# A first stage re-timed on three engines, the last root on GpSimd, and a one-sided closing test

## The chip, the cores and the metric

The kernel runs on one core of a Trainium2 chip. The metric is device time in microseconds (us) of one launch. The engines are PE (TensorE, matmuls), ACT (ScalarE), DVE (VectorE), POOL (GpSimd) and SP (SyncE, which only issues DMAs here). Each has a queue of its own and runs it in order; they meet at semaphores.

## The reference

There are 3125 nodes of 256 features and, with self loops, 53125 edges sorted by target. Cut to what matters (gates i, c, o; f is not used by the result):

```
z   = layernorm(x)                               # 3125 x 256
h   = z @ W_gnn + b_gnn                          # "lines"
x1  = x + segment_sum(h[src], dst) / max(deg, 1)
z2  = layernorm(x1)
xi, xg, xo = z2 @ U_i + b_i, z2 @ U_c + b_c, z2 @ U_o + b_o
# one sequence of 3125 nodes: c' = h*c + sigmoid(xi + h V_i) * tanh(xg + h V_c)
#                             h' = sigmoid(xo + h V_o) * tanh(c')
out = x1 + hs
```

## The kernel before, in words

The 3125 nodes are 25 blocks (steps) of 125 chunks. The recurrence is run on all 125 chunks at once, 25 steps a round, each chunk starting from a guess that the steps before it have made good; at the end a test says whether the last round has moved any start state by more than `STATE_TOL`, and only if it has does a slow exact path run. It does not run here.

The work falls into stages.

1. **Before the first turn**: edges are found, the GNN weight is scaled, PE does dummy matmuls (`keep_busy`).
2. **First stage**, a loop of turns j from 0 to 27 (`BLOCKS + 3`), written out on each engine. In turn j PE transposes block j of z (L1258), makes up to eight counts of edges from one-hot tiles (`count`, L1238), does the products of line j-2 (one matmul for the bias, L1275, six at L1278), and, for a line whose low part ACT makes, subtracts the high part of line j-3 in PSUM (L1284). ACT makes z of the next block (`first_norm`, L899; POOL, L757, makes blocks 11, 13, 15, 17, 19 and from 20 on), copies the transposed z out as its high part (L963), copies two groups of counts out (L934), then writes the low part of line j-3 (L919) and the high part of line j-2 (L914). DVE subtracts to get the low part of the transposed z (`zT_low`, L1716), compares indices to make one-hot tiles (`one_hots`, L1691, used three turns later), and does the moments of x, the roots and the edge keys in chosen turns. "Low parts by DVE" (`low_by_dve`) are lines 21 to 24: DVE takes PSUM minus the high part and PE has no subtraction to do. Edge keys are placed by DVE in turns 4 and 8 and turned by PE at the end of turns 5 and 11.
3. **Sums and gates**, places w from 0 to 649: PE multiplies counts by lines (L1244, L1246), counts the next windows, turns z2 (L1304), makes the gate inputs (L1328) and early steps of the recurrence (L1356). DVE makes the one-hots, up to six tiles ahead of PE (`RING`), then x1, its moments, z2 and the low parts of the weights (L1884, at the places in `UV_LOW`). The inverse root of the variance is made by POOL (`root`, four linked operations from L787 to L791) for turns 0 to 23, and by DVE itself (`last_root`, eight linked operations from L1785) for turn 24. Then come steps 21 to 24 and the last gates, by hand-written places (`LAST_AT`, `LATE_PARTS`).
4. **The recurrence**, 41 steps in two halves, about 1.5 us a half (L1436, L1085, L1908, L1099, L1913).
5. **The end**: the closing test (difference of cells, of states, their squares, one compare with a sum, from L1962 to L2014), the last outputs (L1972), and the last store.

The line that joins most of the engines in the first stage is this wait of PE before the products:

```
t = j - 2
if 0 <= t < BLOCKS:
    pe.wait_ge(zT_ready, t + 1)
    ...
    elif t >= 2:
        pe.wait_ge(line_low_act, lows_act(t - 2))
```

## Time and profile before

| | us |
|---|---|
| median of 3 runs | 456.59 |
| lowest, highest | 456.39, 458.94 |
| the profiled execution, its own time | 457.81 |
| its span, first to last instruction | 455.9 |
| PE, DVE, ACT, POOL busy | 416.8, 341.6, 321.5, 145.9 |

The profiled execution took 1.9 us more than its span shows, and 1.2 us more than the median. Busy shares are means over stages with different limits, so the rows further down are taken stage by stage.

### The profile page before, as it was taken

What the parts mean: (1) busy time and instruction counts of PE and PEld (TensorE: products, weight loads), DVE (VectorE), ACT (ScalarE), POOL (GpSimd) and SP (SyncE); (2) the same over time, 40 slices, a digit from 0 to 9 for tenths busy, and PEclk for the clock granted to TensorE, in tenths of its full rate; (3) what the DMA queues carried; (4) which work ended last, traced back from release to release, by engine and by line L of the source; (5) the groups of instructions that cost most, each with busy time, mean ns of one, the idle gap of its engine ahead of it and who ended that gap; (6) DMA issues with size and microseconds to landing.
All of it is one profiled execution on the core that took longest, in us unless ns stands there. A gap on an engine that the chain in (4) does not pass through costs nothing.

```text
span 455.9 us, 15425 instructions
## 1 busy us (share of the span) xinstructions
PE 416.8 (91%) x6114; PEld 368.5 (81%) x6114; DVE 341.6 (75%) x1095; ACT 321.5 (71%) x906; POOL 145.9 (32%) x249
## 2 busy tenths in 40 slices
PE   4987899999999999999999999998888889999992
PEld 3666787878898999899998989887777778888882
DVE  4989887996997868777786833627577778888885
ACT  1668696577776767667676853564788888888881
POOL 6740420153432435233422412312123222322320
PEclk9989799999999999999999999999999999999997
DMA  8375001331100001000100010000000000210112
GB/s 186 70 156 140 0 1 51 104 104 31 58 2 1 1 4 55 1 2 1 58 2 1 2 39 20 0 3 22 38 4 4 4 3 4 61 51 12 61 60 62
DMA packets 9603, 16.90 MB, mean 37 GB/s; under 512 B 2006, under 2 KB 7451, under 8 KB 9526
## 3 DMA queue, kind: packets, MB, share of 16 engines
q1 hardware_dynamic: 8230, 14.60, 11.0%
q0 software_dynamic: 880, 0.86, 0.9%
q8 instruction: 50, 0.82, 0.8%
q10 hardware_dynamic: 416, 0.39, 0.5%
q14 instruction: 27, 0.22, 0.2%
HBM read 6.23 MB, written 9.61 MB: 35 GB/s over the span
## 4 chain that ended last, share of the span: by engine, by line
PE 64%; DVE 18%; ACT 7%; issue 7%; DMA 2%; POOL 0%; SPq 0%; DVEq 0%; ACTq 0%; POOLq 0%
PE bank L1244 13%; PE bank L1246 13%; PE bank L1328 10%; PE bank L1436 9%; PE bank L1238 6%; PE bank L1356 4%; ACT tc L1099 3%; PE bank L1278 3%; DVE h L1913 3%; DVE hots L1691 3%; DVE h L1950 3%; DVE c_st L1908 2%; DMA x_sb<-in_x_dram 2%; PE bank L1472 1%; PE bank L1304 1%
## 5 line engine op out<-in xcount | busy, mean ns | idle before, releaser
L1238 PE MATMUL bank<-hots 128*128 128x125 f16 x625 | 119.7, 222 | 0.3 <-DVE hots L1691 0.2
L1691 DVE TENSOR_TENSOR hots<-iota,kp 128x1000 f16<-128x1000 f16 x160 | 106.5, 693 | 12.0 <-PE bank L1238 11.9
L1436 PE MATMUL bank<-h,V 128*128 128x62 f16 (+1 forms) x2952 | 101.1, 192 | 13.0 <-DVE h L1913 8.4
L1436 PEld LDWEIGHTS bank<-h,V 128*128 128x128 f16 x2952 | 93.0, 97 | 24.2 <-issue 22.8
L1244 PE MATMUL bank<-h_flat,counts 125*128 125x257 f16 x375 | 96.7, 273 | 0.2 <-ACT counts L934 0.2
L1246 PE MATMUL bank<-h_flat,counts 125*128 125x256 f16 x375 | 95.8, 271 | 0.0
L934 ACT ACTIVATE counts<-bank 125x500 f16<-125x500 f32 x96 | 55.2, 602 | 20.8 <-PE bank L1238 19.7
L1244 PE MATMUL bank<-h_flat,gx 125*128 125x257 f16 x250 | 68.2, 274 | 0.0
L1246 PE MATMUL bank<-h_flat,gx 125*128 125x256 f16 x250 | 67.5, 270 | 0.0
L824 POOL TENSOR_TENSOR hc<-h_flat,c_st 128x126 f32<-128x126 f32 x80 | 34.0, 425 | 95.7 <-DVE c_st L1908 84.9
L1238 PEld LDWEIGHTS bank<-hots 128*128 128x128 f16 x625 | 57.1, 98 | 7.8 <-DVE hots L1691 0.6
L1328 PE MATMUL bank<-z2T,U 128*128 128x250 f16 (+1 forms) x504 | 55.2, 258 | 1.4 <-ACT gx L986 1.1
L934 ACT ACTIVATE gx<-bank 125x500 f16<-125x500 f32 x64 | 37.3, 592 | 18.8 <-PE bank L1238 17.0
L1328 PEld LDWEIGHTS bank<-z2T,U 128*128 128x128 f16 x504 | 43.4, 97 | 6.5 <-issue 2.2
L986 ACT ACTIVATE gx<-bank,gb 128x250 f32<-128x250 f32 (+1 forms) x84 | 32.7, 443 | 22.4 <-PE bank L1328 22.3
L801 POOL TENSOR_TENSOR hc<-h,c_st 128x250 f32<-128x250 f16 x20 | 18.7, 936 | 71.6 <-DVE h L1840 69.9
L1244 PEld LDWEIGHTS bank<-h_flat,counts 125*128 125x128 f16 x375 | 36.6, 98 | 4.8 <-ACT counts L934 0.5
L1913 DVE SCALAR_TENSOR_TENSOR h<-gate,tc 128x126 f16<-128x126 f32 (+1 forms) x80 | 23.6, 294 | 20.6 <-ACT tc L1099 20.6
L787 POOL TENSOR_TENSOR rstd<-var_eps,minus_half 125x1 f32<-125x1 f32 x24 | 18.3, 764 | 63.9 <-DVE var_eps L1556 63.9
L1246 PEld LDWEIGHTS bank<-h_flat,counts 125*128 125x128 f16 x375 | 36.6, 98 | 1.7
L1099 ACT ACTIVATE tc<-c_st 128x126 f32<-128x126 f32 x82 | 25.3, 309 | 15.5 <-DVE c_st L1908 15.4
L1013 ACT ACTIVATE gate<-bank 128x500 f32<-128x500 f32 (+1 forms) x48 | 22.8, 484 | 12.6 <-PE bank L1356 11.9
(185 smaller groups left out, 781.2 us busy)
## 6 DMA issues: line engine op xcount, KB each, us to landing
h_dram<-h_flat SPq DMA_DIRECT2D x1, 3137.2 KB
x_dram<-x_sb SPq DMA_DIRECT2D x5, 625.0 KB
x_sb<-in_x_dram SPq DMA_DIRECT2D x5, 560.0 KB
out_dram<-x_sb SPq DMA_DIRECT2D x4, 560.0 KB
out_dram<-x_sb SPq DMA_DIRECT2D x1, 336.0 KB
x_sb<-in_x_dram SPq DMA_DIRECT2D x5, 65.0 KB
out_dram<-x_sb SPq DMA_DIRECT2D x4, 65.0 KB
gx<-in_L_gnn_weight_dram ACTq DMA_DIRECT2D x1, 256.0 KB, 3.8
```

Source lines behind the costliest of these rows:

```text
L824: nc.gpsimd.tensor_tensor(hc[:, q, :, 0:c1 - c0], h[:, :, c0:c1], c_st[:, c, :, c0:c1], ALU.mult).then_inc(hc_ready[q], 1)
L934: nc.scalar.activation(counts[g % 2][:, :, :, n0:n0 + n], ps_count[group % 3][0:NB, 0:n * KEYS].rearrange("p (n r t) -> p r t n", n=n, r=RUN),
L986: nc.scalar.activation(gx[:, at:at + n, m, :], gates_bank(tile // 2)[:, half * TB * NB:half * TB * NB + n * NB].rearrange("p (s k) -> p s ...
L1013: nc.scalar.activation(gate_w[:, m0:m1, :], early_bank(t, m0)[:, 0:(m1 - m0) * CHUNKS].rearrange("p (m k) -> p m k", k=CHUNKS), ACT.Tanh, ...
L1099: nc.scalar.activation(tc[:, q, :, 0:c1 - c0], c_st[:, c, :, c0:c1], ACT.Tanh, scale=0.5).then_inc(tc_ready[q], 1)
L1238: nc.tensor.matmul(ps_count[group % 3][:, pos * KEYS:(pos + 1) * KEYS], hots[:, ring, 0, g // 2, :, g % 2], hots[:, ring, 1, g // 2, 0:KEY ...
L1244: nc.tensor.matmul(sum_bank(turn)[:, 0:D + 1], of, line[:, s, D:2 * D + 1], start=(s == 0), stop=False, skip_group_check=True)
L1246: return nc.tensor.matmul(sum_bank(turn)[:, 0:D], of, line[:, s, 0:D], start=False, stop=(s == BLOCKS - 1), skip_group_check=True)
L1328: mm = nc.tensor.matmul(at_bank[:, half * TB * NB:half * TB * NB + n_blocks * NB], U16[:, w_part, d, m * P:(m + 1) * P], z2T[:, buf, z_par ...
L1436: mm = nc.tensor.matmul(to[:, m % (2 * HH) * n:(m % (2 * HH) + 1) * n], V16[:, v_part, d, m * P:(m + 1) * P], h16[:, h_part, d, c0:c1], st ...
L1691: nc.vector.tensor_tensor(hots[:, k % RING, :, :, 0:KEYS, :].rearrange("p a h n g -> p (a h) n g"), iota[:, 0:KEYS, :].unsqueeze(1).to_bro ...
L1913: return nc.vector.scalar_tensor_tensor(out=to, in0=gate[:, q, 2 * HH:MT, 0:n], scalar=1.0, in1=tc[:, q, :, 0:n], op0=ALU.add, op1=ALU.mult)
```

## The change

- **Moments sooner**: the statistics of blocks 15 to 24 go from turns 9 to 12 to turns 8 to 11, their root on ACT and DVE from turn 13 to turn 12.
- **Second keys later**: DVE places them in turn 13 (was 8), PE turns them in turn 16 (was 11). The one-hot tiles of turns 6 to 14 are dealt out anew.
- **Products one line behind**: turn 14 does lines 12 and 13, and each turn j after it line j-1. The loop ends a turn earlier. In turn 15 PE does both subtractions ahead of the products.
- **Low parts by turns**: from line 14 on the even lines are DVE's (14, 16, 18, 20, besides 21 to 24).
- **Dummy matmuls**: eight instead of one at the end of turn 4, and two more in each of turns 9 to 16, into the free half of the bank of transposed z, before PE waits for z.
- **One one-hot tile** of the next stage is made in turn 25, and the first three low parts of the weights U move from places 64, 71, 77 to 69, 74, 79.
- **Last root** on POOL like the others; the last turning of z2 on PE goes from place 635 to 632, ahead of step 24's products.
- **Closing test** of one side at a time: six compares (new plus or minus the bound against old) with a sum each, four of the cells, half by half, two of the states; PE adds the six sums. Subtractions, squares and the joint compare go. (Cells and states were squared against the bound before; now either side is tested by itself.)

The diff, cut to its core:

```
-            return t >= BLOCKS - 4
+            return t >= CATCH_UP and t % 2 == 0 or t >= BLOCKS - 4
-        PLACE_KEYS, TURN_KEYS = (4, 8), (5, 11)
+        PLACE_KEYS, TURN_KEYS = (4, 13), (5, 16)
-        HOTS_OF = [0] * HOTS_FROM + [2, 2, 1, 2, 1, 1, 1] + [2] * 11 + [0]
+        HOTS_OF = [0] * HOTS_FROM + [2, 2, 2, 2, 1, 1, 2, 0] + [2] * 10 + [0]
+        CATCH_UP = PLACE_KEYS[1] + 1
+        LINES_END = BLOCKS + 2
+        def lines_at(j):
+            if j < CATCH_UP:
+                return range(max(0, j - 2), max(0, j - 1))
+            return range(j - 2 if j == CATCH_UP else j - 1, min(j, BLOCKS))
...
# ACT, end of a turn
-                if 0 <= j - 3 and not low_by_dve(j - 3):
-                    line_low(j - 3)
-                if 0 <= j - 2 < BLOCKS:
-                    line_high(j - 2)
+                for t in lines_at(j - 1):
+                    if not low_by_dve(t):
+                        line_low(t)
+                for t in lines_at(j):
+                    line_high(t)
...
# PE, start of a turn
+                    if j >= 2:
+                        pe.wait_ge(zT_ready, j - 1)
+                    if HOTS_FROM + HOTS_LATER <= j < WARM_END:
+                        keep_busy(2 * WARM_EACH, bank[5 + j % 2][:, 2 * P:4 * P])
...
# PE, after the counts
+                lines = list(lines_at(j))
+                ahead = 0 if j == CATCH_UP + 1 else 1
+                for t in lines[:ahead]:
+                    line_products(t)
+                for t in lines_at(j - 1):
+                    if not low_by_dve(t):
+                        take_high(t)
+                for t in lines[ahead:]:
+                    line_products(t)
...
# DVE
-                if 9 <= j < 12:
-                    chunk_stats(15 + 3 * (j - 9), 18 + 3 * (j - 9))
-                if j == 12:
+                if 8 <= j < 11:
+                    chunk_stats(15 + 3 * (j - 8), 18 + 3 * (j - 8))
+                if j == 11:
...
-            UV_LOW = {64: 0, 71: 1, 77: 2, 128: 3, 152: 4, 165: 5}
+            UV_LOW = {69: 0, 74: 1, 79: 2, 128: 3, 152: 4, 165: 5}
-                if turn == BLOCKS - 1:
-                    last_root(j)
...
# the closing test on DVE
+                nc.vector.scalar_tensor_tensor(out=near_hits[:, a, :, 0:k1 - k0], in0=new[:, :, k0:k1], scalar=bound,
+                                               in1=old[:, :, k0 + 1:k1 + 1], op0=ALU.add,
+                                               op1=ALU.is_le if bound < 0 else ALU.is_ge, accum_out=near[:, a:a + 1]
+                                               ).then_inc(near_ready, 1)
```

## Rows read from the trace of the kernel before

**Rows 1.** Windows by stage: us, then each engine's busy time, PE clock, DMA share, GB/s.
```profile
26.20:56.50 30.30, 25.84 (x185) 21.26 (x184) 25.58 (x78) 22.00 (x62) 7.99 (x9) 0.83 0.38 90
56.50:72.80 16.30, 15.89 (x154) 13.50 (x152) 12.48 (x25) 16.16 (x44) 3.06 (x6) 1.00 0.01 2
72.80:107.00 34.20, 32.85 (x337) 28.74 (x338) 31.51 (x75) 21.29 (x40) 9.46 (x13) 1.00 0.32 95
107.00:300.00 193.00, 191.04 (x2028) 172.07 (x2027) 136.01 (x327) 130.21 (x289) 68.21 (x102) 1.00 0.04 15
```
**Rows 2.** Windows of 2 us in the first stage, same columns.
```profile
28.00:30.00 2.00, 2.00 (x10) 1.40 (x9) 1.59 (x3) 1.04 (x4) 0.00 (x0) 0.50 1.00 210
...
48.00:50.00 2.00, 1.80 (x9) 1.32 (x10) 1.98 (x5) 1.27 (x3) 2.00 (x3) 0.50 0.00 0
```
**Rows 3.** Waits of PE from 10 to 72 us: in total, times, longest.
```profile
PE bank L1275 <- ACT h_flat L919: 1.8, 6, 0.5
```
**Rows 4.** Timeline of PE, one steady turn (start us, us, operation).
```profile
58.60 0.37 PE L1258 MATMUL bank<-ident,gx 125*128 125x125 f32 x2
...
59.37 0.32 PE L1275 MATMUL bank<-b,ones 33*125 33x256 f16 x1
...
60.34 0.27 PE L1284 MATMUL bank<-h_flat,minus_one 125*125 125x256 f16 x1
60.45 0.38 PE L1258 MATMUL bank<-ident,gx 125*128 125x125 f32 x2
```
**Rows 5.** Timeline of ACT in the same part.
```profile
60.65 0.38 ACT L919 ACTIVATE h_flat<-bank 125x256 f16<-125x256 f32 x1
...
61.19 0.39 ACT L963 ACTIVATE gx<-bank 128x250 f16<-128x250 f32 x1
```
**Rows 6.** Timeline of DVE in the first stage.
```profile
33.43 0.28 DVE L1673 TENSOR_SCALAR gx<-gx 125x256 f32<-125x256 int32 x1
...
35.48 0.67 DVE L1691 TENSOR_TENSOR hots<-iota,kp 128x1000 f16<-128x1000 f16 x1
...
43.79 0.17 DVE L1556 TENSOR_SCALAR var_eps<-mv 125x10 f32<-125x10 f32 x1
...
52.38 0.42 DVE L1716 TENSOR_TENSOR gx<-bank,gx 128x250 f16<-128x250 f32 x1 [1.46 <-ACT gx L963]
...
56.21 0.42 DVE L1716 TENSOR_TENSOR gx<-bank,gx 128x250 f16<-128x250 f32 x1 [0.57 <-ACT gx L963]
```
**Rows 7.** End of the first stage: the first sum on PE, DVE's next tiles.
```profile
72.82 0.28 PE L1244 MATMUL bank<-h_flat,counts 125*128 125x257 f16 x1 [0.24 <-ACT counts L934]
...
73.38 4.21 DVE L1691 TENSOR_TENSOR hots<-iota,kp 128x1000 f16<-128x1000 f16 x7
```
**Rows 8.** Timeline of PE, its one long wait between 80 and 112 us.
```profile
92.86 0.43 PE L1304 MATMUL bank<-ident,z 125*128 125x125 f32 x2 [1.01 <-DVE z L1800]
```
**Rows 9.** Around the last root: POOL's root of the turn before, DVE, PE.
```profile
310.14 0.55 POOL L787 TENSOR_TENSOR rstd<-var_eps,minus_half 125x1 f32<-125x1 f32 x1 [1.00 <-DVE var_eps L1556]
...
311.73 0.19 POOL L791 TENSOR_TENSOR rstd<-rstd,newton 125x1 f32<-125x1 f32 x1
...
317.14 0.15 DVE L1785 TENSOR_SCALAR rstd<-var_eps 125x1 int32<-125x1 int32 x1
...
319.15 0.41 DVE L1800 TENSOR_SCALAR z<-x_sb,mv,rstd 125x256 f32<-125x256 f32 x1
...
85.54 1.09 POOL L787 TENSOR_TENSOR rstd<-var_eps,minus_half 125x1 f32<-125x1 f32 x1 [12.15 <-DVE var_eps L1556]
...
318.88 1.53 PE L1356 MATMUL bank<-h,V 128*128 128x125 f16 x24 [1.40 <-ACT bank L1006]
```
**Rows 10.** The closing test on DVE.
```profile
448.17 0.41 DVE L2007 TENSOR_TENSOR counts<-counts 128x248 f32<-128x248 f32 x1
...
449.39 0.67 DVE L2014 SCALAR_TENSOR_TENSOR counts<-counts,ones 128x496 f32<-128x496 f32 x1
449.99 0.08 DVE L2014 DVE_READ_ACCUMULATOR counts<-counts,ones 128x1 f32 x1
```

More of the change, by code:

```diff
@@ L801, in early_old_part @@
                 nc.gpsimd.tensor_tensor(hc_w, h_start[:, :, :] if t >= SHARP else h16[:, 0, :, :], c_st[:, c_before(t), :, :], ALU.mult).then_inc(e_hc, 1)
-            for turn in range(BLOCKS - 1):
+            for turn in range(BLOCKS):
                 if turn == 3:
@@ L806, in _ @@
                     nc.gpsimd.memset(c_st[:, :, :, :], 0.0).then_inc(e_start, 1)
-                if turn >= 3:
+                if 3 <= turn < BLOCKS - 1:
                     early_old_part(turn - 2)
@@ L949, in _ @@
             first_norm(0)
-            for j in range(BLOCKS + 3):
+            for j in range(LINES_END):
                 if j == 3:
@@ L954, in _ @@
                     deviation(2)
-                if j == 13:
+                if j == 12:
                     deviation(3)
@@ L1247, in sums, with take_high, line_products @@
                                         start=False, stop=(s == BLOCKS - 1), skip_group_check=True)
-            for j in range(BLOCKS + 3):
+            def take_high(t):
+                pe.wait_ge(line_hi, t + 1)
+                nc.tensor.matmul(bank[t % 2][0:NB, 0:D], minus_one[:, :], line[:, t, D:2 * D], start=False,
+                                 stop=True, skip_group_check=True).then_inc(line_left, 1)
+            def line_products(t):
+                pe.wait_ge(zT_ready, t + 1)
+                if t == 0:
+                    pe.wait_ge(later_set, 4)
+                    pe.wait_ge(w_split, 1)
+                    pe.wait_ge(b_split, 1)
+                if t >= 2 and low_by_dve(t - 2):
+                    pe.wait_ge(line_low_dve, lows_dve(t - 2))
+                elif t >= 2:
+                    pe.wait_ge(line_low_act, lows_act(t - 2))
+                nc.tensor.matmul(bank[t % 2][0:NB, 0:D], ones16[:, :], b16[:, :], start=True, stop=False)
+                parts = [(d, w_part, z_part) for w_part, z_part in PRODUCTS for d in range(DH)]
+                for n, (d, w_part, z_part) in enumerate(parts):
+                    mm = nc.tensor.matmul(bank[t % 2][0:NB, 0:D], zT[:, t % 3, z_part, d, :],
+                                          W16[:, w_part, d, :], start=False, stop=(n == len(parts) - 1))
+                mm.then_inc(line_ps, 1)
+            for j in range(LINES_END):
                 if j < BLOCKS:
+                    if j >= 2:
+                        pe.wait_ge(zT_ready, j - 1)
+                    if HOTS_FROM + HOTS_LATER <= j < WARM_END:
+                        keep_busy(2 * WARM_EACH, bank[5 + j % 2][:, 2 * P:4 * P])
                     if z_by_pool(j):
@@ L1288, in _ @@
                 if j < HOTS_FROM + HOTS_LATER:
-                    keep_busy(WARM_EACH)
-                if j == BLOCKS + 2:
+                    keep_busy(WARM_KEYS if j == PLACE_KEYS[0] else WARM_EACH)
+                if j == LINES_END - 1:
                     pe.wait_ge(counted, OUTS)
@@ L1480, in _ @@
                         if (step, d) == (STEPS - 1, 1):
-                            pe.wait_ge(near_ready, 1)
-                            nc.tensor.matmul(ps_one[0:1, 0:1], near[:, :], ones[:, 0:1], start=True, stop=True
-                                             ).then_inc(near_ps, 1)
+                            for a in range(NEAR_TESTS):
+                                pe.wait_ge(near_ready, a + 1)
+                                mm = nc.tensor.matmul(ps_one[0:1, 0:1], near[:, a:a + 1], ones[:, 0:1],
+                                                      start=(a == 0), stop=(a == NEAR_TESTS - 1))
+                            mm.then_inc(near_ps, 1)
                         turn_out(step, d, LAST_ROUND + step + 1 - HIDDEN)
@@ L1728, in uv_extreme @@
                 extreme(n, w[:, :, :, :].rearrange("p d n h -> p (d n h)"))
-            for j in range(BLOCKS + 3):
+            for j in range(LINES_END):
                 if j < BLOCKS:
                     zT_low(j)
-                if j >= 3 and low_by_dve(j - 3):
-                    line_low(j - 3)
+                for t in lines_at(j - 1):
+                    if low_by_dve(t):
+                        line_low(t)
                 if j == 0:
@@ L1762, in _ @@
                     uv_extreme(1, U_sb)
-            for k in range(OUTS, FIRST_HOTS):
+                if j == BLOCKS:
+                    one_hots(OUTS)
+            for k in range(OUTS + 1, FIRST_HOTS):
                 one_hots(k)
@@ L1996, in _ @@
                     if (t, q) == (DONE, 1):
-                        cell_gap()
+                        test_cells(1, -STATE_TOL)
+                        test_cells(1, STATE_TOL)
                     else:
-                        for step, d in out_parts(t, q)[:LAST_OUTS[q]]:
+                        for step, d in out_parts(t, q)[:1]:
                             add_out(step, d)
+                    if (t, q) == (DONE, 0):
+                        test_cells(0, -STATE_TOL)
                     state_next(q, t)
```

85 lines of the change are left out of this document (24 added, 61 removed).

## The prediction

> **What bounds the kernel now.** I read the windows by stage first [rows 1]. From 107 to 300 us PE is busy 191.0 of 193.0 us: nothing but PE counts there, and the change leaves its work alone. So whatever the edits ahead of 107 us win on PE arrives at the end whole, and nothing else of them does. The stretch from 72.8 to 107 has PE at 32.9 and DVE at 31.5 of 34.2 us: two engines close to full, PE slightly ahead. From 56.5 to 72.8 PE and ACT are full (15.9 and 16.2 of 16.3) and DVE is not (12.5). From 26.2 to 56.5 no engine is full (PE 25.8, DVE 25.6, ACT 22.0 of 30.3) and the granted clock averages 0.83: the three wait for each other in turn, and this is where an order can win. The finer windows show the clock at half, 1.2 GHz, at 28 to 30 and 48 to 50 us [rows 2]; the timeline has the matmuls at half speed from about 27.5 to 31 and 48 to 54.7 us, each time after PE had paused again and again. The longest of PE's waits there in total are for ACT's low part, 1.8 us in six [rows 3]; others are for z and for the keys.
>
> **What a steady turn costs.** PE starts turns at 58.60 and 60.45, so 1.85 us; the products begin 0.77 after the turn does, and the subtraction takes 0.11 [rows 4]. ACT goes from its low part at 60.65 to the next copy of z at 61.19, two copies in 0.54 [rows 5], and also has no pause. An even line by DVE takes 0.11 off PE and 0.27 off ACT and gives DVE 0.33. DVE has 16.3 - 12.5 = 3.8 us free in these nine turns [rows 1], so its four added low parts (1.3 us) are hidden by its own pauses; PE's saving is at most 4 x 0.11 = 0.4 us.
>
> **Turns 6 to 13.** Placing the second keys costs DVE 35.48 - 33.43 = 2.05 us in turn 8 [rows 6]; it is moved to turn 13, not saved. The moments move one turn up. Before, the root of the variances stood at 43.79 [rows 6] and ACT waited for it ahead of z 14. Laid out anew by DVE's durations (about 0.33 for a low part of z, 0.59 for a tile, 0.33 for a block's statistics), the same point comes at about 41.0, and z 14 lets PE start turn 14 at about 43.4; without the move it would be later by the same 2 us or so that the root is, less what PE has queued. Part of it (0.6) hangs on the clock staying full at 27.5 to 31: the seven extra dummies are 7 x 0.11 = 0.8 us of PE time ahead of the first key turning. If they don't help, they cost nothing, since PE waits there for DVE's keys.
>
> **The catch-up, turns 14 to 16.** Here something is paid. In turn 14 PE does 12's products, the subtraction of 11, then must wait for ACT's low part of 11 before 13's products (some 0.6 us). In turn 15 ACT does z 16, the copy of z 15 and two copies of counts (about 1.8 us) before low part 12, for which the products of 14 wait. By hand: turn 15 starts at 46.8, PE stands still from 48.0 to 49.5, turn 16 starts at 50.5, and DVE's low part of z 16 comes at 51.4, where it was 52.38; after it come two tiles, a low part and the maximum of U, so that of z 17 comes at about 55.0, where it was 56.21 [rows 6]. DVE is 1.2 us ahead of before. PE is further ahead: turn 19 starts at about 56.5 (58.60 before) with a line less left to do. The second keys' turning (0.45) and 16 dummies (16 x 0.11 = 1.8 us) stand in this part of PE's queue; the copies of the keys stand in ACT's, ahead of high part 15. They lie in PE's pauses, except 0.3 in turn 16.
>
> **To the end of the stage.** From turn 19 PE has, before, lines 17 to 24: 13.8 us to the last product. After it has one line (0.97) and three subtractions (0.3) less: 12.5 us, so the last product and the last five counts end near 69.1. Then there is a new wait. Before, line 24's products came behind the last counts and covered ACT's copies of them, all but 0.24 us [rows 7]. Now the counts come last, and ACT has the high part of line 24 and two count copies to do: about 1.0 us bare. The first sum thus starts near 70.1 instead of 72.82 [rows 7]: **-2.7 us**. DVE has tile 32 done before and starts tile 33 at about 69.8, where it was 73.97: 4.2 us earlier, 1.5 more than PE.
>
> **72.8 to 107 us.** PE's waits here are 1.0 for z [rows 8] and 0.2 for a tile. DVE comes with 1.5 us more lead, and the U low parts behind z rather than ahead of it give 0.66 more. Both waits go: **-1.2 us**. Next is PE itself. DVE can't use more lead: it may be six tiles ahead.
>
> **Last root.** DVE needs 319.15 - 317.14 = 2.0 us for it; POOL needed 311.73 + 0.19 - 310.14 = 1.8 us while DVE worked beside it [rows 9]. POOL's row beside running one-hots has its first operation at 1.09 instead of 0.55 us [rows 9], so the bounds are 1.6 and 2.6 us. DVE only waits while the last root is made, so I take 1.7: z is there 0.2 us sooner, at about 319.3. But PE turns it at place 632 now, ahead of step 24's products, which started at 318.88 [rows 9]; those start at about 319.5, and everything behind them, with the copy of z on ACT queued behind their gate, goes with them: **+0.5 us**, bounds 0 and +0.9. The Trainium skill's page "SBUF — State Buffer", section "SBUF: two separate sides", says that VectorE and GpSimd share a port pair as an exclusive lock, held for a whole instruction, so that one blocks the other. By that rule the long first operation is a wait for one-hots, and an idle DVE costs the root nothing; with the price of the busy row the edit would be +1.4.
>
> **The closing test.** Before, from L2007 at 448.17 to the end of the sum's read at 450.07 are 1.9 us [rows 10]. After, one test of half 0 fits the 0.28 in which DVE waits for the last-but-one tanh; two of half 1 (0.27 each by 122 elements) come ahead of the last state and push it by 0.2, since it waits for ACT anyway. Then 0.26 for half 0 and 2 x 0.39 for the states: the sum is known near 449.45, not 450.07. PE's six one-column products are 0.06 each, five of them early. **-0.5 us**, bounds -0.8 and 0.
>
> **Sum.** -2.7 - 1.2 + 0.5 - 0.5 = -3.9. The layout has about 25 hand-overs between engines in sixteen turns, of which I counted 0.1 to 0.15 each and no collision; I take 0.7 back for that: -3.2. On the profiled time, 457.81, this gives 454.6; that execution lies 1.2 above the median, so the forecast is 456.59 - 3.2 = **453.4**.
>
> **Rivals.** (1) The clock falls again in the catch-up. PE pauses 0.6 and 1.5 us within four, about what it paused before 48 us. For: the fills are 0.21 us a turn only. Against: they come in every turn from 9 on. At half clock a line takes 1.75 instead of 0.97; three or four lines at it cost some 2.4 us, half of it hidden beside DVE: 455.6. (2) No bubble: the catch-up's waits overlap better than by my order, the clock never leaves full, and the stage runs at the load of its fullest engine. Before, DVE had 25.6 + 12.5 = 38.1 us of work in 46.6 [rows 1]; with 1.3 more and 5% of pauses the first sum comes at about 68: another 2 us, 451.3. (3) Slower: with the products one line behind, PE waits in every turn for the low part of z, which comes over ACT and a DVE that is fuller by its low parts. Deciding point: 0.77 us into the next turn [rows 4]. By my layout it arrives 0.2 to 0.8 sooner; if it came 0.5 late in each of the 11 turns, 5.5 us would go and only the closing test and the moments would stay: 457 to 459. (4) The stage is won and not kept: DVE, 92% busy from 72.8 on, sets the pace and PE's lead becomes waits for tiles. Against: DVE comes out 4.2 us sooner. It would give 455.
>
> **How the numbers follow.** My case 0.5, (1) 0.2, (2) 0.18, (3) 0.05, (4) 0.07. A measurement here tells from no change what is over 1%, that is 452.0 and 461.2. Below 452.0 lie nearly all of (2) and a tenth of my case's spread: 0.24. Over 461.2 lies the tail of (3): 0.02. The rest is 0.74. The range goes from the middle of (2), 450.9, to the near end of (3), 456.4.
>
> **What would show it.** First sum near 70 us, and 1 us of ACT's copies ahead of it; PE standing near 48 us for ACT's low part of line 12; clock at full from 26 to 72 us; no wait of PE for z near 90 us; step 24's products about 0.5 later behind their seed than now; DVE's last sum 0.6 us closer to the last cell. The forecast is wrong if the first sum stays behind 71.5 or the clock row shows half speed again, and low if turn 15 has no pause.

## The result, and the profile after

The changed kernel takes 460.08 us (median of 11 runs, 457.51 to 461.69) against 457.84 (11 runs, 456.39 to 459.55) for the kernel before, on the same chip. The ratio is 1.0042, 95% interval 1.0028 to 1.0056: 1.9 us slower, within the 1% that counts as no change, where 3.2 us less were forecast. (The forecast of 453.4 us stood on the 456.59 of the first three runs; 1.25 us of its distance from 460.08 are that base.) The profiled execution of after took 457.74 us, as long as that of before (457.81); it is one of the fastest of its runs. So the two profiles show why nothing was won, and more than them is needed for the 1.9.

Windows by stage of the kernel after (columns as in [rows 1]), then its first stage in windows of 2 us:

```profile
26.20:56.50 30.30, 25.30 (x209) 21.07 (x208) 25.01 (x78) 22.32 (x63) 6.34 (x9) 0.94 0.35 89
56.50:72.80 16.30, 14.60 (x144) 12.32 (x143) 15.55 (x33) 15.40 (x39) 4.41 (x6) 1.00 0.01 3
72.80:107.00 34.20, 33.39 (x348) 29.67 (x347) 30.57 (x75) 21.84 (x40) 8.81 (x12) 1.00 0.31 95
107.00:300.00 193.00, 191.04 (x2030) 172.17 (x2028) 135.22 (x326) 130.56 (x289) 68.25 (x102) 1.00 0.04 15
...
28.00:30.00 2.00, 1.76 (x15) 1.41 (x14) 1.73 (x4) 1.51 (x5) 0.00 (x0) 1.00 1.04 231
...
44.00:46.00 2.00, 2.00 (x12) 1.42 (x10) 1.90 (x6) 1.74 (x5) 1.26 (x2) 0.50 0.00 0
```

From 56.5 us on DVE has the low parts that were meant for it (15.55 us busy for 12.48 in [rows 1]) and PE 1.3 less to do, and from 107 on nothing is changed. The two stretches at half clock of [rows 2] are gone; a new one, 43.8 to 47.2 us, has come. What stands ahead of it is in the timelines. ACT first, then PE (the bracket is the idle time before the operation, and what ended it):

```profile
38.61 0.42 ACT L922 ACTIVATE h_flat<-bank 125x256 f16<-125x256 f32 x1
41.04 0.21 ACT L901 ACTIVATE sd<-var_eps 125x10 f32<-125x10 f32 x1 [2.00 <-DVE var_eps L1580]
41.16 0.36 ACT L971 ACTIVATE gx<-bank 128x250 f16<-128x250 f32 x1
41.41 1.06 ACT L942 ACTIVATE counts<-bank 125x500 f16<-125x500 f32 x2
42.35 0.40 ACT L927 ACTIVATE h_flat<-bank 125x256 f16<-125x256 f32 x1
```
```profile
42.89 0.29 PE L1275 MATMUL bank<-b,ones 33*125 33x256 f16 x1 [2.01 <-ACT h_flat L927]
...
48.04 0.29 PE L1275 MATMUL bank<-b,ones 33*125 33x256 f16 x1 [0.57 <-ACT h_flat L927]
...
51.69 0.29 PE L1275 MATMUL bank<-b,ones 33*125 33x256 f16 x1 [1.43 <-ACT h_flat L927]
...
72.66 0.28 PE L1253 MATMUL bank<-h_flat,counts 125*128 125x257 f16 x1 [1.29 <-ACT counts L942]
```

ACT stands 2.00 us for DVE's variances, and behind its root in the queue are the copy of z, the counts and the low part that PE needs: PE stands the same 2.01 us a moment later, and its clock falls. The root came when the prediction had it: DVE's variances at 40.77 (forecast 41.0), ACT's root at 41.04. (Before, they came at 43.79 and 44.05, and ACT stood 1.16 us.) The first sum comes at 72.66, 0.16 ahead of [rows 7] and not 2.7. Behind it the wait for z of [rows 8] has shrunk by half, and where PE stood at 300.65 in the kernel before (the products of an early step) it stands at 299.61, 1.04 ahead.

The last root: POOL, DVE, PE (compare [rows 9]).

```profile
316.15 0.55 POOL L795 TENSOR_TENSOR rstd<-var_eps,minus_half 125x1 f32<-125x1 f32 x1 [5.26 <-DVE var_eps L1580]
...
317.51 0.19 POOL L799 TENSOR_TENSOR rstd<-rstd,newton 125x1 f32<-125x1 f32 x1
317.65 0.63 POOL L809 TENSOR_TENSOR hc<-h_start,c_st 128x250 f32<-128x250 f32 x1
```
```profile
317.74 0.70 DVE L1812 TENSOR_SCALAR z<-x_sb,mv,rstd 125x256 f32<-125x256 f32 x1 [1.67 <-POOL rstd L799]
```
```profile
318.49 0.43 PE L1326 MATMUL bank<-ident,z 125*128 125x125 f32 x2 [2.05 <-DVE z L1812]
318.75 2.20 PE L1378 MATMUL bank<-h,V 128*128 128x125 f16 x36
...
324.08 0.64 PE L1458 MATMUL bank<-h,V 128*128 128x63 f16 x16 [0.26 <-ACT bank L1081]
```

PE's turning of z waits 2.05 us with step 24's products behind it, and the recurrence starts at 324.08 instead of 324.25: of the lead of 1.04 us, 0.87 are gone. In the recurrence another 1.1 go. Here are two half steps on DVE, before and after:

```profile
329.13 0.14 DVE L2005 CAST open_i<-open_f 1x1 int32<-1x1 f32 x1
329.31 0.29 DVE L1902 SCALAR_TENSOR_TENSOR ig<-gate 128x126 f32<-128x126 f32 x1
```
```profile
328.97 0.14 DVE L2035 CAST open_i<-open_f 1x1 int32<-1x1 f32 x1
329.45 0.29 DVE L1914 SCALAR_TENSOR_TENSOR ig<-gate 128x126 f32<-128x126 f32 x1 [0.34 <-DVE open_i L2035]
```

The same instruction, with the same work done before it, comes 0.48 us behind its neighbour instead of 0.18. It happens four times (near 330, 357, 383 and 407 us). From the first cell (the start of the first `c_st<-hc,ig`) to the last are 121.90 us, before 120.77. Only the closing test gives: the last output ends 0.8 us closer to the last cell than it did.

### The profile page after: what moved, and what is told of

It reads as the page before. It is cut to its first block, busy times and chain, and to the rows that moved or that the text cites. A ratio compares the mean times of both kernels' runs of the same rounds, so it can differ in the third digit from the quotient of the medians.

```text
span 455.9 us, 15476 instructions
## 1 busy us (share of the span) xinstructions
PE 414.6 (91%) x6143; PEld 367.3 (81%) x6143; DVE 340.1 (75%) x1097; ACT 321.0 (70%) x902; POOL 146.3 (32%) x253
## 4 chain that ended last, share of the span: by engine, by line
PE 54%; DVE 27%; ACT 9%; issue 6%; DMA 2%; POOL 0%; SPq 0%; DVEq 0%; ACTq 0%
PE bank L1253 13%; PE bank L1255 13%; PE bank L1350 10%; PE bank L1247 6%; ACT tc L1108 5%; DVE h L1925 5%; DVE h L1962 5%; PE bank L1378 4%; DVE c_st L1920 4%; DVE hots L1715 3%; PE bank L1278 3%; DMA x_sb<-in_x_dram 2%; DVE stats L1608 2%; DVE h_flat L1925 1%; PE bank L1326 1%
## 5 line engine op out<-in xcount | busy, mean ns | idle before, releaser
L1350 PEld LDWEIGHTS bank<-z2T,U 128*128 128x128 f16 x504 | 43.4, 97 | 6.8 <-issue 2.2
```

The lines of the kernel that those rows point to most:

```text
L1350: mm = nc.tensor.matmul(at_bank[:, half * TB * NB:half * TB * NB + n_blocks * NB], U16[:, w_part, d, m * P:(m + 1) * P], z2T[:, buf, z_par ...
```

## The experiments

All kernels were timed against the kernel before on their own chip, five rounds each (three for e6), which gave 5 to 12 runs of each kernel. For each the profile gives three marks on PE and DVE: how long from PE's turning of the first keys (25.82 us before) to the first sum; from there to the first product of the recurrence; and from there to the end of the span. Each is worked out as a difference of two rows' start times, or of the span and a start.

| | first stage | sums and gates | recurrence, end | median us | ratio (95%) |
|---|---|---|---|---|---|
| before | 47.00 | 251.43 | 131.65 | | |
| after | 46.87 | 251.42 | 131.82 | 460.08 | 1.0042 (1.0028 to 1.0056) |
| e1 | 46.84 | 252.85 | 130.85 | 457.88 | 1.0010 (0.9992 to 1.0027) |
| e2 | 45.58 | 251.43 | 131.00 | 456.82 | 0.9986 (0.9974 to 0.9998) |
| e3 | 46.51 | 253.72 | 131.80 | 459.66 | 1.0036 (1.0021 to 1.0052) |
| e4 | 46.74 | 250.56 | 131.57 | 457.70 | 1.0007 (0.9993 to 1.0020) |
| e5 | 46.25 | 251.44 | 131.76 | 457.78 | 1.0001 (0.9988 to 1.0015) |
| e6 | 46.06 | 251.43 | 132.93 | 458.36 | 1.0012 (0.9995 to 1.0029) |
| e7 | 45.33 | 250.55 | 131.26 | 455.22 | 0.9955 (0.9933 to 0.9976) |
| e8 | 43.48 | 250.53 | 131.37 | 452.99 | 0.9895 (0.9870 to 0.9919) |
| e9 | 43.51 | 250.54 | 130.82 | 453.42 | 0.9914 (0.9898 to 0.9931) |
| e10 | 42.36 | 250.86 | 131.41 | 452.25 | 0.9888 (0.9870 to 0.9906) |
| e11 | 44.05 | 250.52 | 130.91 | 453.78 | 0.9924 (0.9910 to 0.9940) |
| e12 | 42.94 | 250.87 | 131.12 | 453.04 | 0.9911 (0.9891 to 0.9931) |
| e13 | 43.96 | 251.42 | 131.37 | 454.82 | 0.9937 (0.9921 to 0.9953) |
| e14 | 42.07 | 250.87 | 131.07 | 452.29 | 0.9884 (0.9867 to 0.9901) |
| e15 | 47.36 | 250.87 | 130.54 | 457.03 | 0.9990 (0.9979 to 1.0001) |
| e16 | 42.20 | 250.85 | 131.24 | 452.59 | 0.9889 (0.9871 to 0.9907) |
| e17 | 42.80 | 251.44 | 130.95 | 452.69 | 0.9916 (0.9896 to 0.9936) |
| e18 | 44.64 | 251.46 | 131.17 | 455.50 | 0.9960 (0.9945 to 0.9975) |

The middle column repeats to 0.03 us wherever the code and the clock are the same; the outer ones scatter (the first mostly with PE's clock, the last by some 0.3). Differences in the first column under 1 us are read from the timelines, not from the column.

**e1, the changed kernel, five DVE instructions later.** The edit, ahead of the recurrence (two such waits make one instruction):

```
+            for _ in range(10):
+                dve.wait_ge(sum_ps, BLOCKS)
```

> The changed kernel, with five more empty instructions on DVE (waits that are long met) just ahead of the recurrence, so that every instruction of the recurrence stands at the same number of DVE's queue as in the kernel before. Nothing of the computation changes. Theory A, places in the queue: DVE is late by some 0.25 us once in 128 instructions, and in the changed kernel that falls where nothing hides it (0.25 us each at about 330, 357, 383, 407 us); moved by five, it falls beside a wait again. Then the cells of the recurrence keep an even pitch, the stretch from the first to the last cell is 1.1 us shorter than in the changed kernel, and its time is 1.1 us under it, or 0.8 over the kernel before to 0.3 under it. Rival B, the recurrence is slower for another reason (the order of the last turn, the phase of the two halves, POOL's last root): the five instructions change nothing, and the pitch still has its four late steps.

The cells took 120.77 us from first to last, the very number of before, and all four late steps were gone. The time was 1.0010 of before where the changed kernel had 1.0042. Theory A holds. The run also showed something else: its recurrence started 252.85 us behind the first sum, 1.43 more than in the profile of after. That is the next run's subject.

**e2, the closing test alone.**

The closing test's part of the change, as it stands in the diff, in the kernel before.

> The kernel before with the one-sided closing test alone. My reading of the two profiles: the changed kernel came into its last microseconds 1.04 us later and ended 0.22 later, so the test gives 0.8 us: time 0.8 under the kernel before. Rival: the gain is only of the changed kernel's late arrival (the last outputs wait for something else that has a place of its own in time), and the test by itself gives 0.0 to 0.3.

The sum of the test is read 1.94 us behind the last cell (before, 2.88), and the last output ends 3.17 behind it (before, 3.91): 0.74 us, close to the 0.8 expected. The ratio says 0.6, the medians 0.4.

**e3, the last root alone, at place 632; e5, the same at place 635.** In both, nine empty instructions on DVE keep the recurrence's numbers.

```
-            for turn in range(BLOCKS - 1):
+            for turn in range(BLOCKS):           # POOL
-                if turn == BLOCKS - 1:
-                    last_root(j)                 # DVE
-  TURN_AT: (576, 588, 625, 635)
+  TURN_AT: (576, 588, 625, 632)                  # e3 alone
```

> The kernel before with the last root on POOL and the last turning of z2 at place 632 alone, and nine empty instructions on DVE ahead of the recurrence for the eight or nine that go with the root, so that the recurrence keeps its numbers in DVE's queue. Theory: the root itself takes no less time than before, the z behind it takes longer than 0.41 us beside POOL's own work, and step 24's products stand behind the turning of z, which waits some 2 us for it: the first products of the recurrence are 0.87 us later against the same seed, time 0.9 over the kernel before. Rival: the delay in the changed kernel came out of what its first stage had done, and alone the edit costs 0.0 to 0.5, as I forecast.

> The kernel before with the last root on POOL, but PE's last turning of z2 left at place 635, behind step 24's products (in the run before this one, of the root alone, it stood at 632, ahead of them), and the recurrence at its old numbers in DVE's queue. Theory P, the place on PE: PE's pause of 2.05 us for z lay open only because the turning stood ahead of the products; now PE does the products while DVE makes z, the first products of the recurrence come 23.6 us behind the 300 us mark as before (not 24.5 or 25.9), PE's clock stays at full from 318 to 324 us, and the time is within 0.3 of the kernel before. Theory R, POOL's root is itself slow and late: z comes 0.6 us later than before, the recurrence starts later by that, and the time is 0.5 to 0.9 over, at either place.

Windows and PE's timeline of e3:

```profile
318.00:320.00 2.00, 0.90 (x14) 0.90 (x15) 0.70 (x1) 0.69 (x2) 0.81 (x3) 1.00 0.32 120
320.00:322.00 2.00, 2.00 (x26) 2.00 (x24) 0.00 (x0) 0.74 (x2) 0.00 (x0) 0.59 0.33 131
322.00:324.00 2.00, 2.00 (x22) 1.88 (x21) 1.16 (x3) 0.50 (x2) 0.00 (x0) 0.56 0.02 7
```
```profile
319.10 0.43 PE L1304 MATMUL bank<-ident,z 125*128 125x125 f32 x2 [2.05 <-DVE z L1798]
319.37 3.12 PE L1356 MATMUL bank<-h,V 128*128 128x125 f16 x36
```

and PE's timeline of e5:

```profile
318.18 1.53 PE L1356 MATMUL bank<-h,V 128*128 128x125 f16 x24 [1.40 <-ACT bank L1006]
319.54 0.39 PE L1304 MATMUL bank<-ident,z 125*128 125x125 f32 x2
```

The pause is 2.05 us, as in the changed kernel, but here PE's clock drops to half (1.2 GHz) behind it, and the 36 products take 3.12 us instead of 2.20. The recurrence starts 2.29 us later than without the edit (253.72 against 251.43), more than either theory had. With the turning back behind the products, PE doesn't stand for z, the clock stays at full, and the edit costs nothing (251.44; ratio 1.0001). So the root on POOL is free, and its place on PE costs 0.87 us in an execution in which the clock holds and 2.3 in one in which it falls. e1 had the fall, the profile of after hadn't. The mean granted clock that is on record for every run fits this: in e3 two of nine runs have 0.987 and took 457.78 and 457.93 us, the other seven have 0.981 to 0.984 and took 458.92 to 460.40. It also fits the changed kernel's runs lying between 457.5 and 461.7 us; how often the clock fell in them, and where, no profile shows.

**e4, the first stage alone; e7, the first stage and the closing test** (the changed kernel with the old last root), both with the recurrence 128 instructions later in DVE's queue than before.

> The kernel before with all edits of the first stage and of the U low parts, with the old root and the old closing test; empty instructions on DVE between places 190 and 400 bring the recurrence to the numbers it had plus 128. Theory: the first sum comes 0.2 us sooner than before, the later waits for z shrink by about 0.9, and 1.0 us arrives at the end: time 1.0 under the kernel before in an execution like the profiled one. In other executions PE's clock may fall more often in turns 13 to 17, since the changed kernel's listed executions had clocks down to 0.982 where the profiled one had 0.990; then it is 0 to 1.5 over. Rival, DVE's empty instructions or the old root eat the 1.0: then the lead is there at 300 us and gone at 324.

> The changed kernel with the last root put back as it was, and the recurrence at its old numbers plus 128: that is the first stage and the closing test together. If parts add up, its time is that of the first stage alone (0.5 over the kernel before, uncertain by 0.6) less 0.6 to 0.8 for the test: 0.1 to 0.3 under the kernel before. If the remaining 1.0 to 1.5 us of the changed kernel sit in something that only the three together have, it stays 1 over.

The same code in the first stage, twice: in e4 the clock fell near 44 us as in the changed kernel, in e7 it held from 24 to 58 us, and the first sum came 1.41 us closer to PE's turning of the first keys (45.33 against 46.74). That is the price of one such fall. Behind the first sum 0.9 us were won in each. e4's median of 457.7 says that the first stage gave nothing in most runs, and e7 was better than the parts added (455.2, where 0.1 to 0.3 under the kernel before was expected). Of e7's eight runs five have a mean clock of 0.993 or more and took 454.67 to 455.40 us, three have 0.991 or less and took 456.55 to 456.96. Why the clock held more often in e7 than in e4 no run shows.

**e6, the kernel before with its recurrence misplaced.**

```
+                if w in range(200, 400, 10):     # DVE
+                    for _ in range(11):
+                        dve.wait_ge(sum_ps, 1)
+            for _ in range(16):                  # ahead of the recurrence
+                dve.wait_ge(sum_ps, BLOCKS)
```

> The kernel before with 123 empty instructions on DVE, 119 of them or so spread over the places 200 to 400, where DVE has time, so that the recurrence stands 123 instructions later in DVE's queue, that is 5 earlier modulo 128, as in the changed kernel. No edit of the change is in it. Theory A: four steps of the recurrence are 0.25 us late as in the changed kernel, the cells take 121.9 us from first to last instead of 120.77, and the time is 1.1 over the kernel before. Rival: late steps come from something that only the changed kernel has, and the cells keep their 120.77; the run with the first stage alone, 128 instructions later, had 120.78.

The cells took 122.15 us; the late steps are at the same four as in the changed kernel, with one more of 0.3 near 398 us. The ratio, 1.0012, is too close to its bounds to say it alone; the pitch of the cells does, together with e1. In e4, 128 instructions later, it was 120.78.

**e8, ACT's root behind its copies.** The kernel of e7 with one step moved:

```
-                if j == 12:
-                    deviation(3)
                 if j + 1 < BLOCKS and not z_by_pool(j + 1):
                     first_norm(j + 1)
...
                 for t in lines_at(j):
                     line_high(t)
+                if j == 12:
+                    deviation(3)
```

> The kernel just named with one step moved on ACT: the root of the last ten variances comes at the end of turn 12, behind the copies and the low and high parts of that turn, not ahead of them. Theory W: ACT's stand of 2.0 us for DVE's variances at 41.0 us is what made PE stand 2.0 us near 42.9 and let its clock fall from 43.4 to 46.9; then both go, PE stands under 1 us at any place before 48, and the first sum comes 1.0 to 2.0 us sooner (near 71), with all of it at the end: time 1.0 to 2.0 under the run before it. Theory D: DVE, with no pause between 35 and 48 us, sets the pace there; the low part of z 12 comes no sooner, PE stands for it instead, and the first sum moves by less than 0.4.

ACT, and then PE, in e8:

```profile
41.25 0.21 ACT L902 ACTIVATE sd<-var_eps 125x10 f32<-125x10 f32 x1
```
```profile
44.89 0.29 PE L1276 MATMUL bank<-b,ones 33*125 33x256 f16 x1 [0.56 <-ACT h_flat L928]
48.53 0.29 PE L1276 MATMUL bank<-b,ones 33*125 33x256 f16 x1 [1.42 <-ACT h_flat L928]
```

The root comes at the same time and waits for nothing, since ACT had its copies to do meanwhile. PE's pause of 2.0 us is gone, that of the catch-up (1.42) is left. The first stage is 1.85 us shorter than in e7 at the same full clock, and 3.39 shorter than in the changed kernel. Theory W, and 2.2 us by the medians, a little more than it had. This kernel takes 452.99 us.

**e9, the changed kernel with three mends** (e1's shift, e5's place, e8's root):

> The changed kernel with three mends: ACT's root of the last ten variances at the end of turn 12, PE's last turning of z2 at place 635 again (the last root stays on POOL), and five more empty instructions on DVE ahead of the recurrence, which give it its old numbers in DVE's queue. If the three losses that the runs so far point to (2 to 3 us of ACT's stand and the clock after it, 0.9 to 2.3 of PE's wait for z at place 632, 1.1 of the late steps in the recurrence) are all that went wrong with the change, and parts add up, its time is that of the run before (453.0, where the root of turn 24 stayed on DVE) within 0.4. If POOL's root costs something of its own, 0.5 to 0.9 more.

453.42, at the edge of that. The three marks are e8's to 0.03 us or less (43.51, 250.54, 130.82), so the profile shows no other loss in the change, and nothing that POOL's root costs. The ratios, 0.9914 and 0.9895 with intervals that overlap, leave room for some tenths.

**e10, without the catch-up,** from e8:

```
-            return t >= CATCH_UP and t % 2 == 0 or t >= BLOCKS - 4
+            return t >= BLOCKS - 4
-        CATCH_UP = PLACE_KEYS[1] + 1
-        LINES_END = BLOCKS + 2
+        CATCH_UP = 99
+        LINES_END = BLOCKS + 3
```

> The run of the stage and the test with ACT's root behind (453.0 us), but with the products two lines behind as in the kernel before up to the end, 28 turns, and low parts by DVE from line 21 on alone; moments, keys, one-hots and dummies as changed. Theory C, the catch-up is what wins: one line (0.97) and four subtractions less at the end, and DVE's four low parts take ACT's place; without it the first sum comes 1.0 to 2.0 us later than 69.5, or about 71, and the time is 454 to 455. Theory K, what wins is the keys at turn 13 and a clock that stays full: PE then pauses nowhere for ACT's low part (0.57 and 1.43 us in the changed kernel), and the first sum moves by under 0.5 either way, time 452.5 to 453.5.

Neither. The first sum came at 67.93, 42.36 behind the turning of the first keys where e8 has 43.48, so 1.12 us sooner:

```profile
50.41 0.29 PE L1276 MATMUL bank<-b,ones 33*125 33x256 f16 x1 [0.43 <-ACT h_flat L928]
...
67.93 0.28 PE L1254 MATMUL bank<-h_flat,counts 125*128 125x257 f16 x1 [0.23 <-ACT counts L943]
```

Of the 1.12 us, 1.06 are the counts laid bare ahead of the first sum (1.29 against 0.23); so the catch-up's bubble just about cancels the line and the subtractions saved at the end. Behind the first sum 0.33 went back (PE waits 0.7 for z there, 0.5 in e8), which leaves 0.8 in the profiles and 0.7 in the medians. The ratios, 0.9888 and 0.9895 with intervals of 0.002 to either side, don't tell the two kernels apart; that e10, e14 and e16 all have 42.1 to 42.4 in the first stage and e8 and e9 43.5 speaks for a real difference. e10 has the lowest median of all, 452.25, level with e14.

**e11, without the added dummies; e12, line 24's products behind the last counts;** both from e8.

```
-        WARM_KEYS, WARM_END = 8, 17              # e11
+        WARM_KEYS, WARM_END = 1, 0
...
+            if j == BLOCKS:                      # e12, in lines_at; LINES_END = BLOCKS + 3
+                return range(0)
+            if j > BLOCKS:
+                return range(j - 2, min(j - 1, BLOCKS))
```

> The run of the stage and the test with ACT's root behind (453.0 us), without the added dummy matmuls: one instead of eight behind turn 4, and none in turns 9 to 16. Theory F, the dummies hold the clock: without them it falls at 27 to 31 us or in the pauses of turns 13 to 16, as in the kernel before, and the first sum comes 0.6 to 2.5 us later, time 453.6 to 455.5. Theory G, the clock holds by the shorter pauses alone, and the dummies stand in PE's way or cost nothing: time 452.5 to 453.1.

> The run of the stage and the test with ACT's root behind (453.0 us), with the products of line 24 in turn 26, behind the last five counts, as in the kernel before, where they cover ACT's copies of these counts. The wait of 1.29 us for ACT's counts ahead of the first sum should shrink. Theory: PE does the products (0.97) in it, and ACT no longer has the high part of line 24 (0.28) ahead of its last copy, so the first sum comes 0.3 to 0.5 sooner, time 452.5 to 452.8. Rival: the low part of line 24 by DVE, which the sums need, comes behind and takes it back: 453.0 to 453.4.

Without dummies the clock fell at 27 to 31 us again, and the run was 0.8 longer (theory F, its low end); in turns 13 to 16 it held. In e12 the wait ahead of the first sum went from 1.29 to 0.21 and the first sum came 0.54 sooner, but 0.34 of that went back behind it, and the time was unchanged. That is the rival's time; the wait that grew is the one for z (0.7 for 0.5), so that the low part of line 24 took it back is not shown.

**e13 to e16, what wins in the first stage.** e13 is the kernel before with the closing test and the dummies; e14, e15 and e16 are e10 without the dummies, with the moments in their old turns, and with the keys in theirs.

```
+                    if HOTS_FROM + HOTS_LATER <= j < 17:             # e13, PE
+                        keep_busy(2, bank[5 + j % 2][:, 2 * P:4 * P])
-                    keep_busy(WARM_EACH)
+                    keep_busy(8 if j == PLACE_KEYS[0] else WARM_EACH)
...
+                if 9 <= j < 12:                                      # e15, DVE
+                    chunk_stats(15 + 3 * (j - 9), 18 + 3 * (j - 9))
+                if j == 13:                                          # ACT, ahead of first_norm
+                    deviation(3)
...
+        PLACE_KEYS, TURN_KEYS = (4, 8), (5, 11)                      # e16
```

> The kernel before with the closing test of the change and its dummy matmuls (eight behind turn 4, two in each of turns 9 to 16), nothing else. Theory C, the clock is most of what the stage can win: the dummies keep PE at full clock through 27 to 31 and 46 to 55 us, the first sum comes near 70 (47.0, 45.4 and 46.5 us behind the first turn's start in the three kernels so far with the old stage; then 43 to 44), and the time is 454 to 455. Theory P, pauses of PE for DVE and ACT set the pace and the clock only follows from them: the clock falls again after 46 us, and the time is 456.0 to 457.0, that of the test alone.

> The best version so far (452.25 us: test, moments and keys as changed, ACT's root behind, products two lines behind), without the added dummies. In the version with the products one behind, leaving them out gave 0.8 more and a clock at half from 27 to 31 us. Theory F, they are worth that here too: 453.0. If they also hold the clock in turns 13 to 16: 454 to 455. If neither, within 0.3 of 452.25.

> The best version with the statistics of blocks 15 to 24 in turns 9 to 12 and their root in turn 13 ahead of z 14, as in the kernel before. Theory M, the order of the root on ACT is what matters, not the turn: ACT again stands for DVE's variances with its copies behind them, PE pauses some 2 us in turn 13 or 14, and the time is 454 to 456. Rival: with the keys in turn 13 DVE is early, the variances come before ACT asks, and it is within 0.5 of 452.25.

> The best version with the second keys placed in turn 8 and turned in turn 11 and the one-hots dealt out as in the kernel before. Theory K, the 2.05 us of DVE in turn 8 push the moments and the low parts of turns 9 to 12, and PE pauses there: first sum 1.0 to 2.0 us later than 67.93, time 453.3 to 454.3. Rival: DVE has the same work in all, and the pause moves only: within 0.5 of 452.25.

In the old order the dummies keep the clock at full and give 2.0 us over e2 (theory C). In e10's order leaving them out costs nothing (e14, +0.0), and in e14's profile the clock stays full. That is not because nothing is there to hold: up to turn 13 e14 and e11 are the same code, and e11's clock fell.

```profile
28.00:30.00 2.00, 2.00 (x9) 1.40 (x8) 1.41 (x3) 1.14 (x5) 0.00 (x0) 0.50 0.99 212
```
```profile
28.00:30.00 2.00, 1.76 (x15) 1.41 (x14) 1.72 (x4) 1.51 (x5) 0.00 (x0) 1.00 0.98 208
```

The first line is e11's, the second e14's. Of the nine profiles without the added dummies four have the clock at half somewhere between 26 and 31 us (before, e2, e11, e17) and five have not (e3, e5, e6, e14, e18); of the eleven with them none has.

The keys give nothing that is clear of the noise (e16: 0.3 by the medians, 0.0 by the ratios). With the moments in their old turns e10 is 4.8 us slower (e15), by another wait than the one I named in theory M; ACT's stand is 1.0 us only, but POOL's z 15 is late:

```profile
42.75 0.43 PE L1294 MATMUL bank<-ident,gx 125*128 125x125 f32 x2 [0.43 <-ACT gx L908]
43.85 0.29 PE L1276 MATMUL bank<-b,ones 33*125 33x256 f16 x1 [0.44 <-ACT h_flat L928]
47.77 0.68 PE L1294 MATMUL bank<-ident,gx 125*128 125x125 f32 x2 [2.49 <-POOL gx L766]
```

PE stands 2.49 us, and its clock is at half from 47 to 54 us. DVE's queue has the cause:

```profile
43.32 0.28 DVE L1698 TENSOR_SCALAR gx<-gx 125x256 f32<-125x256 int32 x1
...
45.30 0.21 DVE L1629 RECIPROCAL rstd<-sd 125x10 f32<-125x10 f32 x1
```

DVE's share of the root stands in turn 13 behind the placing of the second keys, which the change has put into that turn (43.32 to 45.30). So the 4.8 us are the price of the old moments together with the new keys. With the old keys and the dummies the moments are worth 2.2 us (e16 against e13, which differ in the places of the U low parts and in one one-hot tile besides; the first stage alone differs by 1.8).

**e17, the moments alone; e18, the place of ACT's root alone,** both in the kernel before with the closing test. e18 moves `deviation(3)` from the start to the end of turn 13; e17 has DVE's statistics and root a turn sooner and ACT's root at the end of turn 12.

> The kernel before with the closing test of the change, the statistics of blocks 15 to 24 a turn sooner (8 to 11), and ACT's root of them at the end of turn 12; keys, dummies and products as before. Theory M, the moments alone carry what the first stage can win: PE no longer waits for z 14 and 15 (0.84 and 1.08 us in the kernel before), its clock stays full from 46 to 55 us, and the time is 452.3 to 453.3 (the version with the dummies has 452.6). Rival, dummies or moments are each needed for the clock at 27 to 31 us: one dip stays, 453.5 to 454.5.

> The kernel before with the closing test of the change and one move: ACT's root of the last ten variances at the end of turn 13 (before, at its start), with the statistics in their old turns. Theory O, the order in ACT's queue is what matters: ACT's 1.16 us of standing goes, and 2 us or more are won, time 453 to 455. Theory T, the turn matters as well: POOL's z 15 and ACT's z 16 need the root by turn 14 and 15, DVE's deviation comes as late as before or later, PE waits for POOL's z 15 as before, and the time is 456.3 to 457.3, that of the test alone.

e17 has 452.69 us, nearly the whole gain (3.2 us under e2 by the ratios, 4.1 by the medians), though its profile still has a dip of the clock at 26 to 29 us. What the moments give (3.2 to 4.1) and what the dummies give (2.0) don't add: e16 has both and stands 4.2 under e2. e18 has 455.50, 1.3 less than the test alone: between the two theories. Its PE shows what the missing turn costs:

```profile
47.17 0.43 PE L1258 MATMUL bank<-ident,gx 125*128 125x125 f32 x2 [2.36 <-POOL gx L757]
```

## Why the prediction was wrong

**The stage that sets the time was read rightly.** Whatever PE won ahead of 107 us arrived at 300 us whole ([rows 1]; in e8 the 4.2 us between 300.65 and 296.43).

**First sum, forecast 70.1, measured 72.66: the step that failed.** It is the sentence that places the moments: the root at 41.0, z 14 letting PE start turn 14 at 43.4. The root came at 41.04. But the change puts ACT's root a turn sooner *ahead of that turn's copies*, and I never asked what was queued behind it on ACT. There was the low part that PE's next products needed: 2.0 us of PE, and its clock after it (turn 14 starts at 44.47 instead of 43.4; 1.4 us more where the clock falls, by e4 and e7). With the root behind the copies the first sum comes at 69.34 to 69.50 (e9, e8), better than the forecast. The moments are the edit with the largest effect of all, 3 to 4 us in the right place (e17; 2.2 where the dummies are in already), and I had given them three sentences.

**The catch-up, forecast to save PE a line and three subtractions, costs some 0.8 us** (e10). Its pauses I had found (0.6 and 1.5 us; measured 0.57 and 1.43). What I did not do is lay the stage out without the catch-up: its pauses (2.0) and the bare counts (forecast 1.0, measured 1.29) are more than the one line and three subtractions (1.3) that it saves. The net is smaller than their difference, since e10 has pauses of its own (1.8 us for ACT's low part, e8 3.3).

**72.8 to 107 us, forecast -1.2, measured -0.88** (251.43 to 250.55). Right in kind; a wait of 0.5 for z stays, and the one for a tile is 0.3, not gone. In the 40 us behind the first sum PE is idle for 1.33 us before and 0.81 after, which is 0.5 of the 0.88; where the rest lies is not shown.

**Last root, forecast +0.5 (0 to +0.9), measured +0.87 or +2.3.** The order was seen rightly, and that POOL needs about 1.6 us. The upper bound left out what PE does in the 2.05 us: it pauses, and its clock may fall. z took 0.70 us instead of 0.41. The rule of the Trainium skill that the prediction weighed (page "SBUF — State Buffer", section "SBUF: two separate sides": VectorE and GpSimd hold a shared port pair as an exclusive lock, and whichever starts first has it for its whole instruction) speaks of such cases, and the trace agrees in part. POOL's first operation took 0.55 with DVE idle, as the rule would have it, and the long z stands beside POOL's next operation (317.65, 0.63 us). But z begun at 317.74 and held up to that operation's end at 318.28 would take 0.95 us (0.54 of standing and the usual 0.41), and it took 0.70; POOL's times in a profile are rough, and the rows don't settle it.

**Closing test, forecast -0.5 (-0.8 to 0), measured -0.74** (e2).

**The term that was missing: +1.1 us** for late steps in the recurrence, which no edit touches (e1, e6). Taking five instructions away from DVE's queue (the root's nine go, four low parts come) moved a regular delay from operations that wait anyway to ones that don't. Nothing in the sum had a place for that.

**The rivals.** The fall of the clock (0.2) came true, earlier than I had it and for 1.4 us, where I had some 2.4 with half of it hidden (the 455.6 given for it doesn't follow from that; it would be 454.6); the slower one (products waiting for the low part of z) did not: no wait of that kind is in the profile. None of them had the cause.

For the profiled executions the terms are -0.16, -0.88, +0.87, +1.13 and -0.8: +0.2, and the two times differ by -0.1. The 1.9 us between the medians lie in executions that no profile of the changed kernel shows. The one fall of the clock that e1 and e3 show, 1.4 us each, would account for most of it; that stays an inference. For it: six of the eleven runs have a mean clock of 0.982 to 0.987 and took 459.83 to 461.69 us, the others, the profiled one among them, 0.990 to 0.992. Against it as the whole answer: three of those others still took 459.13 to 460.09.

## What to carry to other kernels

When an edit moves an instruction that waits, write down what stands behind it on its own engine; a root that comes at the planned time can still hold back the copies behind it. Put the waiting instruction last in its turn, where the engine has done its other work. The place in the queue alone gave 1.3 us here (e18), the place and the earlier turn 3 to 4 (e17). A pause of PE of 2 us should be priced twice, once as it stands and once with the stretch behind it at half clock (1.4 us more here), and the mean granted clock of each run shows whether the executions differ in it. Weigh each part of a bundle against its absence, and with more than one partner: the place of the last turning cost 0.9 or 2.3 us, the catch-up some 0.8, and the moments were worth 2.2, 3 to 4 or 4.8 us by what stood beside them.

## What the runs showed of the hardware

**DVE is late once in 128 instructions**, by 0.25 to 0.3 us, in a fixed place of its queue. Counted in the kernel's own instructions for DVE, waits included, the late ones of the changed kernel (at 329.45, 356.49, 382.54, 406.44 and 430.32 us) stand exactly 128 apart, and those of e6 have the same remainder by 128. Moved by 5 the delays came out or went in (121.90, 120.77, 122.15 us from first cell to last), moved by 128 they stayed as they were (120.78). Where the instruction there waits for something else the delay is hidden. What it is the trace doesn't say; it has only the regularity.

**PE's clock fell behind pauses of 2.0 us, but not behind each**: the same pause of 2.05 us ahead of the same work had full clock behind it in one execution (after) and half in two (e1, e3), and e4 and e7 differ the same way in the first stage. It also fell behind a pause of 2.36 us (e18) and within one of 2.49 us (e15). Near 28 us it fell in four of nine profiles without the added dummies and in none of eleven with them.
